# A gated cross-attention block with routed experts: the first batch's memsets, stack transfers and output bias are put elsewhere

## The chip, the cores and the metric
The kernel runs on one core of one Trainium2 chip. The metric is the device time of one execution in microseconds (us). Engines are named TensorE (PE in the profile; PEld is its weight load), VectorE (DVE), ScalarE (ACT), GpSimd (POOL) and SyncE (SP). SP, ACT and POOL can issue transfers (SPq, ACTq and POOLq in the rows, or a DMA row of POOL).

## The reference
32 batches of 112 query rows and 375 context rows, 256 wide, float32; 16 heads of 16.

```
x = x + tanh(g_xattn) * attention(layernorm(x), ctx, ctx)      # Wq, Wk, Wv, Wo with biases bq, bk, bv, bo
x = x + tanh(g_ffn) * experts(layernorm(x))                    # router: best 2 of 8, h = silu(x w1) * (x w3), y = h w2
```

## The kernel before
The program is written by hand: each engine has its own list of instructions, and semaphores order them across engines. There are two phases. In the first, the attention of 32 batches runs as a software pipeline of steps from i = -3 to 31. In the second, 63 tiles of 128 routed tokens go through the experts.

A step has 12 slots, k = 0 to 11. In step i the engines work on several batches: a = i + 3 is normed, turned and projected to queries and keys; s = i + 2 gets its values (L1168) and has its queries and keys stacked; c = i + 1 gets its score maxima (L1162 on TensorE, negated maxima by L869 on VectorE); b = i gets its exponents (L1130, L594); e = i - 1 gets its output. Batch 2 doesn't come in step -1 but between the steps -2 and -1 (third_batch). So batch 0 is projected in step -3, batch 1 in step -2, batch 2 behind it, and the maxima of batch 0 are taken in step -1.

Queries and keys are split in a high and a low part for exactness (the tile split, parts KHI, QHI, KLO, QLO). The parts of each head pair are then stacked under one another by transfers inside the SBUF: rows 0 to 31, 32 to 63 and 64 to 95 of the tile stack. Row 96 holds ones against the keys and the negated maxima against the queries. For each of four groups g of heads there are four transfers: from_high makes two (L280, L281), from_low two (L285, L286). For batches from 1 on SyncE issues all 16. For batch 0 SyncE issues 10 and GpSimd's stack_first 6 (L397 to L404). stacked(n) is the count that those who wait for a batch's stack compare with.

What stands around the change:
- GpSimd begins with constants, then the memsets of the ones rows, three of 1 x 3008 elements (L377), then a memset in v_sb (L379), then step -3 with queries(0) (L413 to L427), which masks and splits the queries, then stack_first. Its queue is in order.
- VectorE's first norm: statistics, half (L732), polish1 (L736 to L738) and the normed batch xn (L838). The roots between are on ScalarE (L544, L546).
- TensorE begins with 56 transposes of the identity as a warm-up (L1117), then turns the normed batch (L1247), which ScalarE copies (L610), and makes the queries (L1273) and keys (L1173).
- ScalarE issues the loads of Wo, bv, bo and the router weights, copies values (L567), turned batches (L610), queries (L621) and keys (L616). In third_batch its key copies (L660) wait for the stack of batch 0.
- The output bias: bo_gated = tanh(g) * (bo + bv Wo) is made once, in step -1: VectorE's L876 and L879, TensorE's L1304, VectorE's L883; at the same place the router weights are turned (L1297, L629). GpSimd adds bo_gated to a batch's rows of x one step ahead of their use; TensorE waits for it (s_bog) in step 0, before it writes the bank again.

## Time and profile before

| | us |
|---|---|
| median of 3 runs | 856.07 |
| lowest and highest | 853.0, 857.51 |
| the profiled execution's own time | 855.32 |
| its span in the profile | 853.6 |

| engine | busy us | share of the span |
|---|---|---|
| TensorE matmul | 825.3 | 97% |
| TensorE weight load | 673.7 | 79% |
| VectorE | 486.3 | 57% |
| ScalarE | 422.2 | 49% |
| GpSimd | 476.2 | 56% |

The profile is one execution with a time for each instruction. Matmuls overlap one another, so their row tells how long TensorE had work and not how well it was used. The mean granted clock of TensorE, in shares of 2.4 GHz, is 0.991 over the execution: it has two levels, 1.00 and 0.50 (1.2 GHz). A timeline row says when a group of instructions began, how long it lasted, on which engine and from which line of the kernel, and in square brackets how long the engine had stood idle before it and what ended that.

### The profile page before, as it was taken

How to read it: one execution, taken by the hardware profiler on the slowest of the kernel's cores; microseconds unless marked ns; L12 is line 12 of the kernel's file. 1: busy time of each engine (PE TensorE's matmuls, PEld its weight loads, DVE VectorE, ACT ScalarE, POOL GpSimd, SP SyncE). 2: the span in 40 equal slices, each digit the busy share in tenths (PEclk: the TensorE clock that was granted, in tenths of full speed). 3: DMA queues.
4: the chain of work that ended last, by engine and by line, in shares of the span. 5: the costliest groups of instructions: out<-in, count | busy, mean ns of one | idle time of the engine just before them, and what ended most of it. 6: DMA issues, size and time to landing. Idle time of an engine off the chain costs nothing.

```text
span 853.6 us, 21453 instructions
## 1 busy us (share of the span) xinstructions
PE 825.3 (97%) x7209; PEld 673.7 (79%) x7209; DVE 486.3 (57%) x1163; ACT 422.2 (49%) x1086; POOL 476.2 (56%) x570
## 2 busy tenths in 40 slices
PE   7899999999999999999999999899999999999995
PEld 6578888888888888888888888777777777777773
DVE  4566776777777776777787777655622222222221
ACT  2256665665666566656665666565222222222221
POOL 6454434454555555555655465455777766656652
PEclk8999999999999999999999999999999999999997
DMA  5876777776676677676656664574444443444432
GB/s 153 207 161 168 204 177 174 180 192 156 161 181 155 158 175 172 148 175 164 170 117 158 150 160 111 146 192 74 57 63 62 70 69 62 63 63 63 63 57 31
DMA packets 99842, 112.29 MB, mean 132 GB/s; under 512 B 29276, under 2 KB 81124, under 8 KB 99736
## 3 DMA queue, kind: packets, MB, share of 16 engines
q1 hardware_dynamic: 79720, 92.48, 45.1%
q0 software_dynamic: 18512, 17.60, 13.5%
q8 instruction: 61, 1.00, 0.6%
q10 hardware_dynamic: 1504, 0.85, 0.5%
q14 instruction: 45, 0.37, 0.2%
HBM read 35.48 MB, written 17.53 MB: 62 GB/s over the span
## 4 chain that ended last, share of the span: by engine, by line
PE 85%; DVE 11%; issue 2%; ACT 1%; DMA 1%; POOLq 0%; DVEq 0%; ACTq 0%
PE ps L1417 18%; PE ps L1173 10%; PE ps L1478 10%; PE ps L1162 9%; PE ps L1145 9%; PE ps L1130 8%; DVE negmax L869 6%; PE ps L1168 5%; PE ps L1273 3%; PE ps L1332 3%; PE ps L1436 2%; PE ps L1361 2%; PE ps L1265 2%; PE ps L1247 1%; DVE xa L854 1%
## 5 line engine op out<-in xcount | busy, mean ns | idle before, releaser
L869 DVE TENSOR_REDUCE negmax<-ps 112x2 f32<-112x750 f32 x256 | 240.1, 940 | 124.3 <-PE ps L1162 122.8
L594 ACT ACTIVATE probs<-ps 125x448 f32<-125x448 f32 x384 | 209.5, 547 | 101.8 <-PE ps L1130 95.6
L389 POOL DMA_DIRECT2D stack<-negmax_t x128 | 68.2, 536 | 228.5 <-ACT negmax_t L645 220.8
L1130 PE MATMUL ps<-stack 97*125 97x224 f32 x768 | 189.1, 328 | 0.9 <-ACT probs L594 0.4
L1130 PEld LDWEIGHTS ps<-stack 97*125 97x125 f32 x768 | 127.4, 188 | 28.1 <-ACT probs L594 1.5
L1162 PE MATMUL ps<-stack 96*112 96x376 f32 x512 | 136.7, 348 | 7.7 <-DVE negmax L869 5.4
L505 POOL DMA_INDIRECT out_dram<-y,idx x63 | 100.5, 1595 | 69.5 <-issue 34.4
L689 ACT ACTIVATE silu<-ps 128x352 f32<-128x352 f32 x63 | 29.3, 465 | 184.4 <-PE ps L1417 184.4
L1081 DVE TENSOR_TENSOR h<-silu,ps 128x352 f32<-128x352 f32 x63 | 32.8, 521 | 144.6 <-PE ps L1417 144.4
L1168 PE MATMUL ps<-wv_sb,ctx_t 128*125 128x256 f32 x384 | 100.0, 382 | 0.4 <-DVE split L859 0.4
L1173 PE MATMUL ps<-ctx_t,wk_sb 128*128 128x375 f32 x256 | 93.7, 489 | 0.7 <-ACT q_raw L654 0.7
L1478 PE MATMUL ps<-w_sb,h_t 128*128 x378 | 92.3, 380 | 0.7 <-ACT h_t L695 0.7
L1478 PEld LDWEIGHTS ps<-w_sb,h_t 128*128 128x128 f32 x378 | 71.7, 190 | 20.1 <-issue 0.9
L1417 PE MATMUL ps<-w_sb,xg_t 128*128 x252 | 84.9, 458 | 0.0
L1162 PEld LDWEIGHTS ps<-stack 96*112 96x112 f32 x512 | 72.0, 177 | 15.0 <-DVE negmax L869 13.9
L1145 PE MATMUL ps<-probs,v_sb 125*17 125x112 f32 x3072 | 79.8, 260 | 0.0
L1145 PEld LDWEIGHTS ps<-probs,v_sb 125*17 125x17 f32 x3072 | 71.7, 98 | 8.0 <-ACT probs L594 5.4
L496 POOL DMA_INDIRECT xg<-xn_scratch,idx x63 | 62.5, 992 | 25.4 <-issue 17.2
L567 ACT ACTIVATE v_sb<-ps 125x256 f32<-125x256 f32 x96 | 36.5, 381 | 78.8 <-PE ps L1145 76.6
L409 POOL DMA_INDIRECT slot_table<-pay,slots_i x64 | 64.2, 1003 | 15.3 <-issue 13.6
L1168 PEld LDWEIGHTS ps<-wv_sb,ctx_t 128*125 128x125 f32 x384 | 66.6, 187 | 6.8 <-DVE split L859 0.6
L1173 PEld LDWEIGHTS ps<-ctx_t,wk_sb 128*128 128x128 f32 x256 | 46.7, 195 | 18.3 <-issue 1.7
(221 smaller groups left out, 1216.9 us busy)
## 6 DMA issues: line engine op xcount, KB each, us to landing
stack<-split SPq DMA_DIRECT2D x252, 150.0 KB, 2.7
ctx_t<-in_ctx_dram SPq DMA_DIRECT2D x32, 375.0 KB, 3.9
stack<-split SPq DMA_DIRECT2D x127, 94.0 KB, 2.5
stack<-split SPq DMA_DIRECT2D x127, 56.0 KB, 2.1
out_dram<-xa SPq DMA_DIRECT2D x32, 112.0 KB, 3.5
xn_scratch<-xn SPq DMA_DIRECT2D x32, 112.0 KB, 3.3
xa<-in_x_dram SPq DMA_DIRECT2D x7, 448.0 KB, 5.6
w_sb<-in_L_ffn_w_dram SPq DMA_DIRECT2D x16, 176.0 KB, 3.1
```

The lines of the kernel that those rows point to most:

```text
L389: gp.dma_start(dst[:, :, SKP + SQ * h:SKP + SQ * h + SQ], negmax_t[4 * h:4 * h + 4, half, :].bitcast(f32)).then_inc(s_nmrow[half][c % NSLO ...
L409: gp.indirect_dma_start(table, bass.IndirectOffsetOnAxis(ap=slots_i[:, u % 2, GB * k + j:GB * k + j + 1], axis=0), pay[:, UNITS[u][j], k, ...
L505: gp.indirect_dma_start(out, bass.IndirectOffsetOnAxis(ap=idx[:, t % NI, 0:1], axis=0), y[:, t % NY, :], None, compute_op=ALU.add).then_in ...
L594: act.activation(probs[:, n % NP, :], ps[0:KW, EXPB + k % 2, 0:4 * SQ], ACT.Exp).then_inc(s_exp, 1)
L869: dve.tensor_reduce(negmax[:, half, :, p4], ps[0:SQ, m1:m2 + 1, 0:SK], axis=AX.X, op=ALU.max, negate=True).then_inc(s_max, 1)
L1130: last = pe.matmul(ps[0:KW, EXPB + k % 2, QW * m:QW * m + QW], stack[:, place_of(b), p, KW * ch:KW * ch + KW], stack[:, place_of(b), p, SK ...
L1145: last = pe.matmul(ps[32 * j:32 * j + HD + 1, PVB, SQ * g:SQ * g + SQ], v_sb[:, b % NSLOT, ch, head, :], probs[:, (12 * b + 3 * g + ch) % ...
L1162: last = pe.matmul(ps[0:SQ, max_banks(c, t)[h], 0:SKP], stack[0:ONE_ROW, place_of(c), t, SKP + SQ * h:SKP + SQ * h + SQ], stack[0:ONE_ROW, ...
L1168: last = pe.matmul(ps[0:KW, bank, 0:EMB], ctx_t[:, s % NSLOT, n, KW * ch:KW * ch + KW], wv_sb[:, n, :], start=(n == 0), stop=(n == DC - 1))
L1173: last = pe.matmul(ps[:, bank, 0:SK], wk_sb[:, n, P * m:P * m + P], ctx_t[:, a % NSLOT, n, :], start=(n == 0), stop=(n == DC - 1))
L1417: last = pe.matmul(ps[:, bank, 0:F], xg_t[:, t % NS, k, :], w[k][:, bass.ds(e, 1), :].rearrange("p e f -> p (e f)"), start=(k == 0), stop= ...
L1478: last = pe.matmul(ps[:, YB, 0:EMB], h_t[0:n, c, :], w2_sb[0:n, c, bass.ds(e_o, 1), :].rearrange("p e d -> p (e d)"), start=(c == 0), stop ...
```

## The change
- GpSimd waits for the first normed batch (s_xn at 1) before it writes the ones rows.
- The stack of batch 0 goes out on three queues: SyncE issues 8 transfers, GpSimd 5, and ScalarE 3 in a new stack_first of its own, right behind its step -3. It waits there for the low part of the queries of batch 0 (s_qlo) and its high keys (s_khi). The counts in stacked and in the waits for s_stack_gp follow.
- The output-bias chain and the turning of the router weights go from step -1 to step 0 on TensorE, VectorE and ScalarE; GpSimd's first three adds of bo_gated all come in step 1, and TensorE's wait for s_bog moves to step 1.
- TensorE makes four more identity transposes in step -3, between the turning of the first batch and its query matmuls.

```diff
         def stacked(n):
-            return 256 * (n // NSLOT + 1) - (96 if n % NSLOT == 0 else 0)
+            return 256 * (n // NSLOT + 1) - (80 if n % NSLOT == 0 else 0)
...
+                    def low_keys(g):
+                        rows, pr = slice(32 * g, 32 * g + 32), slice(DC * g, DC * g + DC)
+                        sp.dma_start(dst[32:64, pr, :], src[rows, :, KLO:KLO + KQ]).then_inc(s_stack[s % NSLOT], 16)
...
                         for g in range(2):
-                            from_low(g)
+                            low_keys(g)
...
             gp.wait_ge(s_split0, 1)
+            gp.wait_ge(s_xn, 1)
             for n in range(NSLOT):
                 gp.memset(stack[ONE_ROW:ONE_ROW + 1, n, :, 0:SKP].bitcast(f32), 1.0).then_inc(s_one, 1)
...
                 gp.dma_start(dst[32:64, pr, :], src[rows, :, KLO:KLO + KQ]).then_inc(s_stack_gp, 16)
-                gp.dma_start(dst[64:96, pr, :], src[rows, :, KHI:KHI + KQ]).then_inc(s_stack_gp, 16)
...
-                if c is not None and c > 0:
-                    if c == 1:
-                        gp.wait_ge(s_xn, 1)
+                if c is not None and c > 1:
+                    if c == 2:
                         gp.wait_ge(s_bog, 1)
-                        gp.tensor_tensor(xrow(0), xrow(0), bo_gated[:, :], ALU.add).then_inc(s_xb, 1)
+                        for n in range(2):
+                            gp.wait_ge(s_xn, n + 1)
+                            gp.tensor_tensor(xrow(n), xrow(n), bo_gated[:, :], ALU.add).then_inc(s_xb, 1)
...
-                    if k == 7 and i == -1:
+                    if k == 7 and i == 0:
                         act.wait_ge(s_wr_ps, 1)
...
+            def stack_first():
+                src, dst = split[:, 0, :, :].bitcast(f32), stack[:, place_of(0), :, :].bitcast(f32)
+                act.wait_ge(s_qlo, 1)
+                act.wait_ge(s_khi, DC)
+                for g in range(3):
+                    rows, pr = slice(32 * g, 32 * g + 32), slice(DC * g, DC * g + DC)
+                    act.dma_start(dst[64:96, pr, :], src[rows, :, KHI:KHI + KQ]).then_inc(s_stack[0], 16)
+
             for i in range(FIRST, LAST):
                 step(i)
+                if i == FIRST:
+                    stack_first()
...
-                    if k == 5 and i == -1:
+                    if k == 5 and i == 0:
                         dve.wait_ge(s_tanh, 1)
...
-                    if k == 9 and i == -1:
+                    if k == 9 and i == 0:
                         dve.wait_ge(s_bo_ps, 1)
...
-                            if i == 0:
+                            if i == 1:
                                 pe.wait_ge(s_bog, 1)
...
                         if a == 0:
+                            for n in range(4):
+                                pe.transpose(ps[:, 2, P * n:P * n + P], ident[:, :], ident[:, :])
                             pe.wait_ge(s_wq, 32)
...
-                    if k == 7 and i == -1:
+                    if k == 7 and i == 0:
                         pe.wait_ge(s_wr, 16)
-                        pe.wait_ge(s_nm_t, 1)
+                        pe.wait_ge(s_nm_t, 3)
...
-                    if k == 8 and i == -1:
+                    if k == 8 and i == 0:
                         pe.wait_ge(s_bvb, 1)
```

## Rows read from the trace of the kernel before

**Rows 1.** The page, part 1: busy us, share of the span, instructions.
```profile
PE 825.3 (97%) x7209; PEld 673.7 (79%) x7209; DVE 486.3 (57%) x1163; ACT 422.2 (49%) x1086; POOL 476.2 (56%) x570
```

**Rows 2.** Timeline, GpSimd, VectorE and ScalarE: start us, us, engine, line, operation, idle before.
```profile
2.10 7.72 POOL L377 MEMSET stack<- 1x3008 f32 x3
7.29 1.28 ACT L540 ACT_TABLE_LOAD   x1
8.33 1.52 DVE L732 TENSOR_SCALAR half<-mv 112x4 f32<-112x4 f32 x1
10.95 0.41 DVE L838 TENSOR_SCALAR xn<-xa,mv,rstd 112x256 f32<-112x256 f32 x1
...
43.00 0.17 DVE L732 TENSOR_SCALAR half<-mv 112x4 f32<-112x4 f32 x1
```

**Rows 3.** Timeline of TensorE from 1 to 26 us.
```profile
1.61 7.99 PE L1117 MATMUL ps<-ident 128*128 128x128 f32 x56 [1.61 <-POOL ident L364]
...
12.37 2.02 PE L1273 MATMUL ps<-xn_t,wq_sb 128*128 128x112 f32 x8 [0.54 <-ACT xn_t L610]
14.18 4.95 PE L1173 MATMUL ps<-ctx_t,wk_sb 128*128 128x375 f32 x8
...
21.96 1.04 PE L1273 MATMUL ps<-xn_t,wq_sb 128*128 128x112 f32 x8
...
24.40 1.43 PE L1173 MATMUL ps<-ctx_t,wk_sb 128*128 128x375 f32 x4
```

**Rows 4.** Windows: mean; busy (count) of PE, PEld, DVE, ACT, POOL; clock; DMA share, GB/s.
```profile
4.00:5.00 1.00, 1.00 (x7) 1.00 (x6) 0.73 (x1) 0.00 (x0) 1.00 (x2) 1.00 0.89 261
5.00:6.00 1.00, 1.00 (x11) 1.00 (x10) 0.00 (x0) 0.00 (x0) 1.00 (x1) 1.00 1.16 279
12.00:13.00 1.00, 0.64 (x3) 0.67 (x4) 0.28 (x1) 0.22 (x1) 0.00 (x0) 0.50 1.15 219
18.00:19.00 1.00, 1.00 (x4) 0.58 (x3) 0.53 (x1) 0.00 (x0) 0.52 (x1) 0.65 0.18 54
25.00:26.00 1.00, 1.00 (x5) 0.68 (x4) 0.00 (x0) 0.14 (x1) 1.00 (x3) 1.00 1.09 224
```

**Rows 5.** Timeline of GpSimd: the v_sb memset and the queries of batch 0.
```profile
9.88 0.36 POOL L379 MEMSET v_sb<- 125x144 f32 x1
15.20 0.56 POOL L422 TENSOR_TENSOR q_msk<-q_raw,q_mask 128x224 f32<-128x224 f32 x1 [4.97 <-ACT q_raw L621]
...
17.39 1.14 POOL L426 TENSOR_TENSOR split<-q_msk,split 128x448 fp32r<-128x448 f32 x1
```

**Rows 6.** Timeline: SyncE's first and last issue for batch 0, and who waited.
```profile
19.83 0.77 SPq L280 DMA_DIRECT2D stack<-split  x1
...
27.68 0.60 SPq L286 DMA_DIRECT2D stack<-split  x1
...
30.50 0.57 ACT L660 ACTIVATE split<-ps,bk_sb 128x375 fp32r<-128x375 f32 x1 [0.16 <-DMA stack<-split]
```

**Rows 7.** Timeline of ScalarE behind its step -3.
```profile
20.03 0.39 ACT L567 ACTIVATE v_sb<-ps 125x256 f32<-125x256 f32 x1 [0.29 <-PE ps L1168]
20.88 0.36 ACT L610 ACTIVATE xn_t<-ps 128x224 f32<-128x224 f32 x1 [0.47 <-PE ps L1247]
```

**Rows 8.** Step -1's end: timeline rows, and transfers of L389 to landing.
```profile
38.27 1.09 POOL L389 DMA_DIRECT2D stack<-negmax_t  x2 [4.39 <-ACT negmax_t L645]
38.38 1.09 PE L1304 MATMUL ps<-wo_sb,o_t 128*112 128x256 f32 x4 [0.36 <-ACT wr_t L629]
39.85 0.94 DVE L869 TENSOR_REDUCE negmax<-ps 112x2 f32<-112x750 f32 x1 [0.84 <-PE ps L1162]
40.71 0.48 DVE L883 SCALAR_TENSOR_TENSOR bo_gated<-ps,tanh_g,bo_gated 112x256 f32<-112x256 f32 x1
42.38 0.45 PE L1130 MATMUL ps<-stack 97*125 97x224 f32 x2
...
DMA to landing us min/median/max: 1.8/2.9/4.5
```

More of the change, by code:

```diff
@@ L415, in queries @@
                 if a == 2:
-                    gp.wait_ge(s_stack_gp, 96)
+                    gp.wait_ge(s_stack_gp, 80)
                 if a >= 2:
@@ L656, in third_batch @@
                 act.wait_ge(s_stack[0], stacked(0))
-                act.wait_ge(s_stack_gp, 96)
+                act.wait_ge(s_stack_gp, 80)
                 for m in range(DC):
@@ L1152, in maxes @@
                 if t == 0 and c == 0:
-                    pe.wait_ge(s_stack_gp, 96)
+                    pe.wait_ge(s_stack_gp, 80)
                 if c == B - 1 and t in (3, 4, 5, 6):
```

## The prediction
> **What bounds the kernel now.** I read the page first. TensorE's matmuls cover 97% of the span [rows 1]. So nearly every microsecond by which the first real step of TensorE moves is carried to the end, and the only open question is the start, where the change works. There I read the timelines engine by engine from 0 to 45 us, then the granted clock in 1 us windows, then the transfers.
>
> Three facts of the start matter. First, VectorE waits for GpSimd: the tiny half op of L732 takes 1.52 us while the third memset of the ones rows runs and ends just after it, and 0.17 us later in the kernel [rows 2]. The three memsets take 7.72 us together. Second, TensorE's warm-up ends at 1.61 + 7.99 = 9.60 us [rows 3], the first normed batch is ready only at 10.95 + 0.41 = 11.36 [rows 2], and after that pause the granted clock is 0.50, the 1.2 GHz level, from 12 to about 18.6 us [rows 4]. The first eight query matmuls cost 2.02 us instead of 1.04, the first eight key matmuls 4.95 [rows 3]. Third, GpSimd is free from 9.88 + 0.36 = 10.24 us on [rows 5], so that it takes the first queries at 15.20, as soon as they exist, and has both parts in split at 17.39 + 1.14 = 18.53 [rows 5].
>
> **The change part by part.**
>
> *Ones rows behind the normed batch.* On VectorE this gives back 1.52 - 0.17 = 1.35 us, of which ScalarE's table load, which ends at 7.29 + 1.28 = 8.57 [rows 2], leaves 1.3: the batch is normed at about 10.07 instead of 11.36. TensorE's pause shrinks from 1.8 to 0.5 us, so I expect the clock to stay at 2.4 GHz; that is worth (2.02 - 1.04) + (4.95 - 2 x 1.43) = 3.1 us [rows 3]. Together 4.4 us, early.
>
> But GpSimd's queue is strictly in order, and this is the step on which the forecast turns. The added wait on the normed batch holds back the three memsets, then the v_sb memset (0.36 us), then the queries of batch 0. Memsets: 10.1 to 17.8. v_sb: to 18.25. Queries: 3.33 us (15.20 to 18.53 [rows 5]), to 21.6. VectorE's second and third norming (0.41 us each [rows 2]) are of the kind that took turns with the memsets; each may add up to 0.4 to this row, so I take 22.0, with ends 21.6 and 22.4. The queries of batch 0 are therefore 3.5 us later than before.
>
> *Stack on three queues.* SP issues 8 transfers of batch 0 instead of 10, GpSimd 5 instead of 6, ScalarE 3 instead of none. The SP issues take 0.77 us at first and 0.60 and a gap later, from 19.83 to 28.28, and the last landed at about 30.5, when the copy of L660 went [rows 6]. All now starts when the queries are there, at 22.0. Lower bound for the landing: 8 issues of 0.65 and 2.7 to land, 8 us, so 30. Upper bound: as long as before, 10.7 us, so 32.7. The DMA engines were full already: share 1.09 at 224 GB/s [rows 4]. I take 9.5 us: 31.5, one later than before; it doesn't bound as long as the third batch is later too (below).
>
> The Trainium skill (Trainium Kernel Development and Optimization, Key Constraints) says that transfers issued from SP, ScalarE and GpSimd run on the same 16 DMA engines, and that issuing from several only saves issue time. The full share agrees; by the rule the three queues bring at most the two issues that SP is rid of, 1.3 us by the rows, and by itself it would change no sign.
>
> What the third queue costs is on ScalarE. Its stack_first stands between the first step and the second and waits for the queries. Queued behind it are the value copy of L567 and the copy of the turned second batch of L610, for which TensorE's queries of batch 1 wait. Before, they ran at 20.03 and 20.88 [rows 7]. Now: wait until 22.0, three issues of 0.8, 0.65 and 0.65, then 0.39 and 0.36 [rows 7] with small gaps: done at 25.05. The query matmuls of batch 1 start at 25.1 instead of 21.96: **3.1 us later**. All of the early 4.4 us lies in front of this wait and is lost in it: TensorE has the keys of batch 0, its first values and the first half of batch 1's keys done at about 19 and then stands for some 6 us.
>
> *The clock again.* Before, a pause of 1.8 us with little around it brought the 1.2 GHz level; one of 6 us will too. Work that began at 12.37 had the full clock at about 18.6; the warm-up, which began at 1.61, did 7 transposes in the microsecond from 4 and 11 in that from 5 [rows 3, 4]. By these two rises, 3.4 and 6.3 us after the first matmul, I take the clock back at 28.5 to 31.4. At half speed that costs 1.7 to 3.1 us, less what TensorE's short gaps up to 24.40 swallow (the eight queries end at 23.00 [rows 3], the values between take about 0.9 and leave 0.5), up to 1. I take 1.4, ends 0.7 and 3.1. The four identity transposes, 1/11 us each, lie in the 0.54 us in which TensorE waits for the turned batch [rows 3]: 0. If the clock were low there they would take 4/7 = 0.57, which is the gap as well; their help to the clock is in front of the same wait and lost with the rest.
>
> *Stack of batch 1.* It needs both keys of batch 1 low, at about 31, and SP free (28): 31 + 16 x 0.645 + 2.7 = 44; TensorE wants it (42.67 before) at 46 or later. Hidden by about 2 us.
>
> *Output-bias chain one step later.* Out of step -1 go two transposes, four matmuls (1.09 us and 0.36 of waiting for ScalarE [rows 8]), and VectorE's bo work, 0.48 us of it at the end. VectorE's idle 0.84 in front of the reduction at 39.85 goes. Upper bound of the gain: 0.84 + 0.48 + 0.36 = 1.7. But the next thing, the exponents of batch 0, needs the negated maxima in the stack: issued at 38.27 and done at 39.36, landing 1.8 to 4.5 us later; the exponents went at 42.35 [rows 8]. That landing was at 40.6 to 42.4 and doesn't move with this part. So the gain is 0 to 1.7; since the DMA engines are full here I take 0.5. Into step 0 goes the same work: TensorE there is nearly full, so 1.1 us, ends 0.8 and, with VectorE's last op of 0.48 on the way too, 1.6. GpSimd's adds go from two to three in the next step (0.75 us more), ahead of maxima that come 4 us later: 0. Net +0.6, ends -0.9 and +1.6.
>
> **Sum**, against the profiled execution (855.32 us, span 853.6, 1.7 outside): + 3.1 + 1.4 + 0.6 = + 5.1, so 860.4. That execution is 0.75 us below the median of the runs shown (856.07, runs from 853.0 to 857.51), so on the median it would be 861.2. I say 860.6.
>
> **Rivals.**
> - *The clock comes back at once or is never lost.* For: the old pause was followed by a nearly idle microsecond. Against: 6 us of nothing. + 3.1 + 0 to 0.6 - 0.9: 857.5 to 859.
> - *The clock stays low through the third batch.* The third batch has gaps of 0.4 to 0.9 us, and in the one recovery seen it took work without gaps. Another 8 query and 8 key matmuls at half speed, 3.5 us, and some of step -1: 863 to 866.
> - *The stack alone decides.* Before, the copy of L660 and the queries of batch 2 went just after the stack of batch 0 had landed (30.50 [rows 6]). If that landing was the true limit, only its own move counts: -0.4 to +2.2 us and the bias chain: 855 to 857.5. Against: the chain that ended last goes through keys and their copies there, and the keys were ready with it.
> - *Faster: GpSimd gets to the queries in time.* The place is GpSimd's queue. If the memsets behind the batch took at most 2 us instead of 7.72 (because their length before came from sharing with VectorE), queries and keys would meet at about 17, ScalarE would be rid of its issues at 19, and the queries of batch 1 would start at 19.7, 2.3 us earlier, at full clock: 852 to 854. It decides where GpSimd ends the ones rows before 13 us. Against: the memsets fill their 7.72 us evenly, also from 5 to 6 us, where VectorE ran nothing (VectorE 0.00, GpSimd 1.00 [rows 4]).
>
> **How the numbers follow.** Forecast 0.46 (858.8 to 862.5), clock kept 0.15, clock low long 0.18, stack alone 0.12, faster 0.09. The range leaves out the faster rival and the far end of the long one: 855.5 to 865.5. A measurement of this kernel can tell about 0.5%, 4.3 us, here up to 860.3: above it lie somewhat under two thirds of the forecast and all of the long rival, 0.48; below 851.8 lie the faster rival's far end and what I haven't seen, 0.07; within, 0.45.
>
> **What would show it.** In the changed kernel: the half op of L732 at about 0.17 us and the first normed batch at 10.1 (right: first part); the three memsets from 10.1 to 17.8 and the first queries of GpSimd at 18.3, not 15.2 (the step on which all turns); ScalarE's issues starting near 22 and L610's second copy near 24.7; TensorE idle from about 19 to 25; granted clock 0.50 somewhere from 20 to 30; the exponents of batch 0 at about 46.5. If GpSimd's queries come before 16 us, or ScalarE's copies before 21, the prediction is wrong on the side of faster.

## The result: slower, by more than predicted

| | us |
|---|---|
| changed kernel, median of 4 runs | 870.17 |
| lowest and highest | 868.57, 876.01 |
| kernel before, on the same chip | 856.79 |
| ratio, with its 95% interval | 1.0179 (1.013 to 1.0229) |
| the profiled execution's own time, its span | 876.01, 874.3 |

The change costs about 13 to 15 us. The prediction was 860.6 with a range of 855.5 to 865.5: the sign was right, the size was a third of the real one, and the time lies outside the range. Repeated with the experiments, the changed kernel gave 868.62 against 855.26, a ratio of 1.0152 (1.0122 to 1.0182), 13.0 us.

The page of the changed kernel, part 1 (busy us, share of the span, instructions), answers to [rows 1]:

```profile
PE 832.7 (95%) x7213; PEld 679.9 (78%) x7213; DVE 487.7 (56%) x1163; ACT 422.1 (48%) x1086; POOL 476.0 (54%) x569
```

TensorE is 7.4 us busier, though only four small instructions were added: the same work ran for longer at the low clock (mean granted clock 0.981 here, 0.991 before). The rest of the loss is waiting. Where both came in is seen by laying the marks of TensorE's timelines side by side. The turn of the maxima (L1178 before, L1193 in the changed kernel) comes once in every step:

| mark on TensorE | before | changed | later by |
|---|---|---|---|
| queries of batch 1 | 21.96 | 24.89 | 2.93 |
| maxima of batch 0 turned, step -1 | 37.06 | 41.37 | 4.31 |
| maxima of batch 1 turned, end of step -1 | 42.09 | 44.70 | 2.61 |
| first exponents (L1130, L1145) | 42.38 | 49.49 | 7.11 |
| next turn, end of that step's work | 50.32 | 58.63 | 8.31 |
| next turn, one step on | 58.31 | 72.41 | 14.10 |

To 540 us the difference stays at 14.4. It is 20.7 at the end of this execution (spans 874.3 and 853.6). The last 6.3 us belong to this execution, the longest of the four, more than to the change: the repeated kernel's profile has a span of 867.1, 13.5 above 853.6. So there are four pieces: +4.31, then -1.70, then +5.70, then +5.79, together 14.10.

**The first piece, +4.31.** Timeline of the changed kernel from 6 to 42 us, one engine after another (start us, us, engine, line, operation, count, idle before and what ended it), the part that answers to [rows 2], [rows 3], [rows 5] and [rows 7]:

```profile
8.39 0.17 DVE L747 TENSOR_SCALAR half<-mv 112x4 f32<-112x4 f32 x1
...
9.89 0.41 DVE L853 TENSOR_SCALAR xn<-xa,mv,rstd 112x256 f32<-112x256 f32 x1
10.81 2.37 DVE L853 TENSOR_SCALAR xn<-xa,mv,rstd 112x256 f32<-112x256 f32 x1 [0.51 <-PE ps L1262]
...
10.43 7.83 POOL L382 MEMSET stack<- 1x3008 f32 x3 [8.39 <-DVE xn L853]
18.79 0.56 POOL L426 TENSOR_TENSOR q_msk<-q_raw,q_mask 128x224 f32<-128x224 f32 x1
...
22.14 2.02 ACTq L673 DMA_DIRECT2D stack<-split  x3
24.20 0.38 ACT L572 ACTIVATE v_sb<-ps 125x256 f32<-125x256 f32 x1 [7.80 <-issue]
24.48 0.35 ACT L615 ACTIVATE xn_t<-ps 128x224 f32<-128x224 f32 x1
...
24.89 2.05 PE L1290 MATMUL ps<-xn_t,wq_sb 128*128 128x112 f32 x8 [6.05 <-ACT xn_t L615]
```

Read down, it is the chain of the prediction. The half op is fast and the first batch is normed at 10.30, but the memsets now follow it and push GpSimd's queries to 18.79 (15.20 before). They are done at 20.98 + 1.13 = 22.11. ScalarE's last copy ends at 16.40. It then waits 5.74 us, issues its three transfers from 22.14 on, and copies again at 24.20. The profile gives the 7.80 us between the two copies as idle and calls them "issue", since an issue isn't counted as work; the three issues lie within them. Then come the copy of the turned batch and, 0.06 us behind it, TensorE, after 6.05 us idle and at the low clock: eight queries take 2.05 us, not 1.04 [rows 3].

**The second and third piece, -1.70 and +5.70.** The same timeline around the end of step -1, GpSimd, SyncE and TensorE, and the transfers issued from 42.5 to 43.2 us (KB each, median us to landing), which answer to [rows 8]:

```profile
41.37 0.26 PE L1193 MATMUL ps<-ident,negmax 112*8 112x112 f32 x1
44.70 0.26 PE L1193 MATMUL ps<-ident,negmax 112*8 112x112 f32 x1 [0.23 <-DVE negmax L884]
49.49 0.73 PE L1145 MATMUL ps<-stack 97*125 97x224 f32 x2 [4.53 <-DMA stack<-negmax_t]
...
41.72 0.59 SPq L221 DMA_DIRECT2D ctx_t<-in_ctx_dram  x1
42.35 0.49 SPq L228 DMA_DIRECT2D xa<-in_x_dram  x1
...
42.58 1.08 POOL L394 DMA_DIRECT2D stack<-negmax_t  x2 [4.40 <-ACT negmax_t L650]
...
stack<-negmax_t POOLq DMA_DIRECT2D x2, 1.8 KB, 5.3
```

Between the two turns lie 3.33 us instead of 5.03: the bias chain is gone and has given back 1.70, all that the prediction had as its upper bound. But then TensorE waits 4.53 us for two transfers of 1.8 KB. SyncE has issued its next two loads, 375 and 448 KB, just ahead of them. In the kernel before GpSimd's pair was issued from 38.27 to 39.36 [rows 8], and the loads began 0.41 and 1.05 us behind its start:

```profile
38.68 0.59 SPq L221 DMA_DIRECT2D ctx_t<-in_ctx_dram  x1
39.32 0.50 SPq L228 DMA_DIRECT2D xa<-in_x_dram  x1
```

The order has turned round, because the maxima moved by 4.3 us and SyncE's loads by only 3.0. Of the 5.70 us, 4.50 have come in when the exponents start (7.11 - 2.61); the other 1.20 come in up to the next turn, where TensorE works at half speed at first (below).

**The fourth piece, +5.79.** Step 0 in the changed kernel, VectorE, GpSimd and TensorE from 58 to 73 us:

```profile
59.69 0.35 DVE L891 TENSOR_SCALAR bo_gated<-bo_sb,tanh_g 112x256 f32<-112x256 f32 x1
60.07 0.47 DVE L894 TENSOR_SCALAR o_t<-head_rows,bv_col 128x112 f32<-128x112 f32 x2
60.45 2.48 DVE L751 TENSOR_TENSOR lnt<-lnr 112x4 f32<-112x4 f32 x1
62.96 0.16 DVE L752 TENSOR_TENSOR lnt<-lnt,half 112x4 f32<-112x4 f32 x1
63.15 0.99 DVE L753 SCALAR_TENSOR_TENSOR rstd<-lnt,lnr 112x4 f32<-112x4 f32 x1
64.17 0.94 DVE L884 TENSOR_REDUCE negmax<-ps 112x2 f32<-112x750 f32 x1
...
60.78 0.57 POOL L426 TENSOR_TENSOR q_msk<-q_raw,q_mask 128x224 f32<-128x224 f32 x1
61.31 0.56 POOL L427 TENSOR_TENSOR split<-q_raw,q_mask 128x224 fp32r<-128x224 f32 x1
61.83 0.56 POOL L426 TENSOR_TENSOR q_msk<-q_raw,q_mask 128x224 f32<-128x224 f32 x1
62.34 0.55 POOL L427 TENSOR_TENSOR split<-q_raw,q_mask 128x224 fp32r<-128x224 f32 x1
62.97 1.15 POOL L430 TENSOR_TENSOR split<-q_msk,split 128x448 fp32r<-128x448 f32 x1
...
65.17 0.59 PE L1177 MATMUL ps<-stack 96*112 96x376 f32 x2 [1.48 <-DVE negmax L884]
66.80 0.97 PE L1177 MATMUL ps<-stack 96*112 96x376 f32 x2 [0.82 <-DVE negmax L884]
```

In the kernel before, the polish and the first masking op stood so:

```profile
51.38 0.15 DVE L736 TENSOR_TENSOR lnt<-lnr 112x4 f32<-112x4 f32 x1
52.49 0.57 POOL L422 TENSOR_TENSOR q_msk<-q_raw,q_mask 128x224 f32<-128x224 f32 x1
```

The polish of L751 handles 4 numbers in each of 112 rows. It takes 0.15 us in the kernel before and 2.48 us here. It ends at 62.93, when GpSimd's fourth masking op ends (62.34 + 0.55 = 62.89). L753 takes 0.99 and ends at 64.14, with GpSimd's next op (64.12). In the kernel before the polish had just passed in front of the masking. The bias ops, 0.35 + 0.47 us ahead of it, push it against the masking, the next reduction comes only at 64.17, and TensorE stands for it. That is 5.54 us behind the turn at 58.63; in the kernel before the same reduction starts at 52.34, 2.02 us behind its turn. So 3.52 of the 5.79 us have come in there. The other 2.27 come in behind it, most of that time at the low clock.

**The clock.** Windows of the changed kernel (mean; busy and count of PE, PEld, DVE, ACT, POOL; granted clock; DMA share, GB/s), answering to [rows 4]:

```profile
22.00:30.00 8.00, 5.12 (x17) 4.12 (x18) 1.51 (x5) 2.08 (x6) 5.34 (x11) 0.57 0.79 196
46.00:54.00 8.00, 4.24 (x16) 3.67 (x16) 1.71 (x3) 1.83 (x5) 0.85 (x2) 0.57 0.92 211
66.00:74.00 8.00, 7.20 (x38) 5.97 (x42) 4.14 (x7) 2.71 (x6) 0.54 (x1) 0.57 0.42 93
584.00:600.00 16.00, 12.67 (x148) 10.14 (x147) 4.47 (x20) 6.35 (x18) 6.47 (x7) 0.89 0.64 156
```

A mean of 0.57 over 8 us is 0.50, the 1.2 GHz level, for most of it. In windows of 1 us the clock is at 0.50 from about 22.4 to 29.0, from 46.0 to 52.9 and from 66.5 to 73.2 us, some 7 us each time. The first two stretches begin within the long waits (6.05 and 4.53 us), so TensorE works at half speed for only 4.1 and 3.4 us of them; the third begins behind the two shorter waits (1.48 and 0.82), and in it TensorE works almost all the time. The last row lies where attention hands over to the experts, and belongs to the late 6.3 us. The kernel before had one such stretch at its start [rows 4] and none from 20 to 76 us.

### The profile page after: what moved, and what is told of

Same layout as the page of the kernel before. It is cut to its first block, busy times and chain, and to the rows that moved or that the text cites. A ratio compares the mean times of both kernels' runs of the same rounds, so it can differ in the third digit from the quotient of the medians.

```text
span 874.3 us, 21463 instructions
## 1 busy us (share of the span) xinstructions
PE 832.7 (95%) x7213; PEld 679.9 (78%) x7213; DVE 487.7 (56%) x1163; ACT 422.1 (48%) x1086; POOL 476.0 (54%) x569
## 4 chain that ended last, share of the span: by engine, by line
PE 82%; DVE 10%; DMA 2%; issue 2%; POOL 2%; ACT 1%; ACTq 0%; POOLq 0%; DVEq 0%
PE ps L1434 17%; PE ps L1495 9%; PE ps L1177 9%; PE ps L1160 9%; PE ps L1188 9%; PE ps L1145 7%; PE ps L1183 6%; DVE negmax L884 5%; PE ps L1290 3%; PE ps L1349 3%; PE ps L1453 2%; PE ps L1378 2%; PE ps L1280 1%; DVE xa L869 1%; PE ps L1262 1%
## 5 line engine op out<-in xcount | busy, mean ns | idle before, releaser
L1145 PE MATMUL ps<-stack 97*125 97x224 f32 x768 | 191.2, 332 | 5.3 <-DMA stack<-negmax_t 4.5
L1145 PEld LDWEIGHTS ps<-stack 97*125 97x125 f32 x768 | 129.1, 190 | 32.9 <-issue 5.7
L1183 PE MATMUL ps<-wv_sb,ctx_t 128*125 128x256 f32 x384 | 104.3, 395 | 0.0
L1188 PE MATMUL ps<-ctx_t,wk_sb 128*128 128x375 f32 x256 | 91.7, 480 | 0.7 <-ACT q_raw L659 0.7
L1183 PEld LDWEIGHTS ps<-wv_sb,ctx_t 128*125 128x125 f32 x384 | 69.3, 194 | 6.8
L1434 PEld LDWEIGHTS ps<-w_sb,xg_t 128*128 128x128 f32 x252 | 47.3, 188 | 16.9
```

The lines of the kernel that those rows point to most:

```text
L1145: last = pe.matmul(ps[0:KW, EXPB + k % 2, QW * m:QW * m + QW], stack[:, place_of(b), p, KW * ch:KW * ch + KW], stack[:, place_of(b), p, SK ...
L1183: last = pe.matmul(ps[0:KW, bank, 0:EMB], ctx_t[:, s % NSLOT, n, KW * ch:KW * ch + KW], wv_sb[:, n, :], start=(n == 0), stop=(n == DC - 1))
L1188: last = pe.matmul(ps[:, bank, 0:SK], wk_sb[:, n, P * m:P * m + P], ctx_t[:, a % NSLOT, n, :], start=(n == 0), stop=(n == DC - 1))
L1434: last = pe.matmul(ps[:, bank, 0:F], xg_t[:, t % NS, k, :], w[k][:, bass.ds(e, 1), :].rearrange("p e f -> p (e f)"), start=(k == 0), stop= ...
```

## The experiments

Three causes were on trial, called A, B and C. **A:** the wait in front of the memsets delays GpSimd's queries and, through ScalarE's new wait, the second batch. **B:** the loads of SyncE, issued ahead of GpSimd's pair of maxima, delay the landing. **C:** the bias chain in step 0 meets GpSimd's masking. Every kernel below computes all that the reference asks for; only places and orders differ. Ratios are to the kernel before, measured on the same chip in the same rounds, with their 95% interval. I turn a ratio into us with the median of the kernel before beside it, some 855 to 861.

**The ones rows alone** (kernel before, one line added).

```diff
             gp.wait_ge(s_split0, 1)
+            gp.wait_ge(s_xn, 1)
             for n in range(NSLOT):
```

> The kernel before with one edit: GpSimd waits for the first normed batch before it writes the ones rows. Theory A (GpSimd's queue order): the memsets run from 10.4 to 18.3 us and the low part of the queries of batch 0 is ready at 22.1 instead of 18.53. ScalarE isn't held here, so TensorE's queries of batch 1 start early, near 18.6 instead of 21.96; but the stack of batch 0 starts 2.3 us later (22.2) and lands near 32.8, the key copies of the third batch wait for it, TensorE stands some 4 us, and the first reduction of step -1 starts at 34.7 to 36.5 instead of 33.09. Total +2 to +5 us, and up to +9 if the loads that SyncE issues behind the stack of batch 1 get ahead of the negated maxima. Rival (the memset costs only together with ScalarE's new transfers): the early gain of 3 us stays, total -3 to 0 us.

Measured: 861.09 us, ratio 1.0043 (1.002 to 1.0067), 3.7 us slower. Timeline, GpSimd, ScalarE and TensorE:

```profile
18.66 0.56 POOL L423 TENSOR_TENSOR q_msk<-q_raw,q_mask 128x224 f32<-128x224 f32 x1
...
32.11 1.04 ACT L661 ACTIVATE split<-ps,bk_sb 128x375 fp32r<-128x375 f32 x2 [3.49 <-DMA stack<-split]
...
47.44 0.45 PE L1131 MATMUL ps<-stack 97*125 97x224 f32 x2 [0.80 <-DMA stack<-negmax_t]
```

GpSimd's queries come as late as in the whole change. Without ScalarE's new wait the second batch goes early (its queries at 18.80), but the key copies of the third then wait 3.49 us for the late stack, so the delay comes out a little further on. There the granted clock falls too: it is at 0.50 from about 31 to 45 us. The first reduction, at 33.75, is only 0.7 us later than before, but the first exponents are 5.1 us later. The wait in front of the memsets is a cost by itself, whichever queue carries the stack.

**The three queues alone** (kernel before with stack_first on ScalarE, SyncE 8, GpSimd 5).

```diff
+            def stack_first():
+                src, dst = split[:, 0, :, :].bitcast(f32), stack[:, place_of(0), :, :].bitcast(f32)
+                act.wait_ge(s_qlo, 1)
+                act.wait_ge(s_khi, DC)
...
+                if i == FIRST:
+                    stack_first()
```

> The kernel before with one part of the change: stack of batch 0 on three queues (SyncE 8, GpSimd 5, ScalarE 3). Theory B (order of issues): ScalarE waits only until 19.7 for its own key copies and issues for 2 us, so that the first reduction of step -1 starts 0.6 to 1 us later. SyncE is free 1.3 us earlier, so its loads of context 3 and of x are issued near 38.1 to 38.8, in front of GpSimd's transfers of the negated maxima (38.9 instead of 38.27), and these land 5 to 6 us after issue instead of within 3: the first exponents 3 to 5 us later, with low clock behind it. Total +3 to +7 us. Rival (landing time doesn't depend on that order): total +0.5 to +1 us.

Measured: 859.72 us, ratio 1.0035 (1.0016 to 1.0053), 3.0 us slower. Timeline around 36 us, all engines:

```profile
36.24 0.59 SPq L221 DMA_DIRECT2D ctx_t<-in_ctx_dram  x1
...
36.45 1.09 POOL L393 DMA_DIRECT2D stack<-negmax_t  x2 [4.27 <-ACT negmax_t L648]
...
36.87 0.50 SPq L228 DMA_DIRECT2D xa<-in_x_dram  x1
...
43.96 0.52 PE L1143 MATMUL ps<-stack 97*125 97x224 f32 x1 [3.44 <-DMA stack<-negmax_t]
```

This is B with neither of the others. SyncE, rid of two issues, is at its loads 0.2 us ahead of GpSimd's pair, and the first exponents wait 3.44 us. Step 0 is untouched (53.37 to 61.37, 8.0 us). The edit that was meant to shorten the stack costs through what SyncE does next. The clock is at 0.50 from about 42 to 49 us, within and behind this wait.

**The bias chain alone** (kernel before, the conditions `i == -1` of the bias and the router turned to `i == 0`, GpSimd's adds as in the change).

```diff
-                    if k == 5 and i == -1:
+                    if k == 5 and i == 0:
                         dve.wait_ge(s_tanh, 1)
```

> The kernel before with one part of the change: the output-bias chain and the turning of the router weights in step 0 instead of -1. Theory C (VectorE and GpSimd get in each other's way in step 0): the last reduction of step -1 ends 1.7 us earlier, the first exponents come 0 to 1.7 us earlier; in step 0 the polish of the norm (two operands in SBUF), pushed back by 0.8 us of bias work, meets GpSimd's masking of the queries and lasts 2 to 3.5 us instead of 0.5; step 0 becomes 3 to 5 us longer. Total +2 to +5 us. Rival (only its own work moves): step 0 +1.1 to +1.6 us, total -0.6 to +1.6 us.

Measured: 863.65 us, ratio 1.0073 (1.0047 to 1.0099), 6.2 us slower, the dearest part. Timeline, VectorE and TensorE:

```profile
52.00 2.38 DVE L737 TENSOR_TENSOR lnt<-lnr 112x4 f32<-112x4 f32 x1
...
40.19 0.45 PE L1131 MATMUL ps<-stack 97*125 97x224 f32 x2 [1.76 <-DMA stack<-negmax_t]
```

The 1.70 us gained in step -1 (turns at 34.84 and 38.17) turn into 1.76 us of waiting for the maxima, as the prediction had feared. The prediction didn't reckon with what follows: behind this wait the clock is at 0.50 from about 42 to 48 us, and from the exponents to the next turn it takes 9.90 us (40.19 to 50.09), not 7.94. Step 0 takes 50.09 to 62.85, 12.76 us instead of 7.99, and the polish takes 2.38. So two thirds of this part's loss are step 0, and the rest is the low clock behind the wait. The three parts alone cost 3.7 + 3.0 + 6.2 = 12.9 us, the whole 13.0; each of the three carries some 2 us of uncertainty, so the close agreement is chance in part.

**The loads behind the maxima** (changed kernel, SyncE's loop in step -1).

```diff
+                if i == -1:
+                    sp.wait_ge(s_nmrow[0][0], 32)
                 if a is not None and NSLOT - 1 <= a < B - 1:
```

> The changed kernel, and SyncE waits in step -1 for the landing of batch 0's first negated maxima before it issues the loads of context 3 and of x. Theory B (the 1.8 KB transfers landed 6.2 us after issue because 823 KB of loads were issued just ahead of them): they land within 3.5 us, TensorE's stall of 4.5 us before the first exponents shrinks to at most 1.5, the granted clock stays at 1.00 there; 4 to 6 us faster than the changed kernel in the same runs. Rival (GpSimd's transfers land late by themselves, or because of the stack transfers of batch 1): stall of 3.5 us or more as before, no gain.

Measured: 862.86 us, ratio 1.005 (1.0031 to 1.0068). Timeline, GpSimd and SyncE, and the transfers issued from 43.5 to 44.8 us:

```profile
43.62 1.09 POOL L396 DMA_DIRECT2D stack<-negmax_t  x2 [4.40 <-ACT negmax_t L652]
...
45.81 0.37 SPq L221 DMA_DIRECT2D ctx_t<-in_ctx_dram  x1
...
stack<-negmax_t POOLq DMA_DIRECT2D x2, 1.8 KB, 1.6
```

The pair lands in 1.6 us instead of 5.3, the exponents go at 45.92 with no wait, and the clock is kept there. From turn to turn it is 45.74 to 53.97, 8.23 us, exactly as in the kernel before (42.09 to 50.32). So the third piece is B's. Step 0 stays bad (13.78 us), as it should. Against 1.0152 this is 1.0%, 8.7 us, of which the timeline shows 5.7; I expected 4 to 6. The two ratios are from different chips and their intervals allow for it.

The edit holds back SyncE's whole queue, the next stack transfers included (46.80 instead of 42.96), so this run alone doesn't tell the loads from those. The two kernels before it do: in both the next stack transfer is issued more than 1 us behind the pair's start (37.49 against 36.45, and 37.59 against 36.05). Only the loads stand otherwise: the first 0.21 us ahead of the pair with the three queues, 0.29 us behind it with the bias chain moved. From the pair's issue to the exponents it is 7.51 us in the one and 4.14 in the other.

**The changed kernel again, and the polish ahead of the bias ops.** The first is the reference point for the polish and for the copy of the ones rows, on one chip.

> The changed kernel itself, for a ratio beside the others on the same chip. All theories: 8 to 15 us slower than before; the stall of 4 to 5 us before the first exponents and the polish of 2.5 and 1 us in step 0 are there again. The extra 5 us between the attention and the experts, seen once, is expected in few executions.

Measured: 868.62 us, ratio 1.0152, with a wait of 3.72 us in front of the first exponents and a step 0 of 12.75 us (58.72 to 71.47). In the second, polish1 was put in front of the bias block of VectorE's slot k = 5.

```diff
+                    if k == 5 and i % GB == 0 and 1 <= i // GB + 1 < NG:
+                        polish1(i // GB + 1)
                     if k == 5 and i == 0:
```

> The changed kernel with VectorE's polish of the norm put in front of the bias work in step 0. Theory C (the polish, with two operands in SBUF, was pushed by 0.8 us of bias work into GpSimd's masking of the queries and waited for it): the polish takes 0.16 us an operation, step 0 is 3 to 4 us shorter, and the clock doesn't fall around 66 us; 4 to 6 us faster than the changed kernel. Rival (the bias work itself, 1.2 us on VectorE and 1.1 on TensorE, makes step 0 long): at most 1 us faster.

Measured: 869.96 us, ratio 1.0167 (1.0137 to 1.0196): no gain at all. Timeline, VectorE and TensorE:

```profile
59.19 0.15 DVE L751 TENSOR_TENSOR lnt<-lnr 112x4 f32<-112x4 f32 x1
...
60.16 2.51 DVE L896 TENSOR_SCALAR o_t<-head_rows,bv_col 128x112 f32<-128x112 f32 x2
...
62.73 2.00 PE L1321 MATMUL ps<-wo_sb,o_t 128*112 128x256 f32 x4 [2.04 <-DVE o_t L896]
```

The polish is back at 0.15 us and my expectation fell: now the bias op stands beside GpSimd's masking (60.30 to 62.40) and takes 2.51. TensorE waits 2.04 us for it, its next scores are late, and with them VectorE's next reduction, at 67.39 after 3.87 us of waiting. Step 0 takes 58.14 to 71.51, 13.4 us. What is in conflict is then not one op but the place: 0.82 us more of VectorE's work has to fit in front of GpSimd's masking of batch 3. Step -1 had no such masking. The run was meant to part the conflict from the work itself (the rival) and doesn't, since the conflict only went over to another op.

**The ones rows by a copy** (changed kernel, no wait on the first batch, no long memset: GpSimd sets 8 x 376 elements, and SyncE copies them three times).

```diff
-            gp.wait_ge(s_xn, 1)
-            for n in range(NSLOT):
-                gp.memset(stack[ONE_ROW:ONE_ROW + 1, n, :, 0:SKP].bitcast(f32), 1.0).then_inc(s_one, 1)
+            gp.memset(one_src[:, :], 1.0).then_inc(s_one_src, 1)
...
+            for n in range(NSLOT):
+                sp.dma_start(stack[ONE_ROW:ONE_ROW + 1, n, :, 0:SKP].bitcast(f32), one_src[:, :]).then_inc(s_one, 16)
```

> The changed kernel with the ones rows made in another way: GpSimd writes a small source of 8 x 376 ones (about 0.35 us instead of 7.8) and SyncE copies it into row 96 three times. Theory A (GpSimd's memsets in front of the queries hold ScalarE): GpSimd takes the queries at 12.8, SyncE and ScalarE start the stack at 16.5, TensorE's queries of batch 1 start at 19 to 20 instead of 24.9 and with full clock; the first reduction of step -1 starts 6 to 8 us earlier, at 29.5 to 31. What is left of the loss is B and C. 6 to 8 us faster than the changed kernel. Rival (the stack's transfers on a full DMA bound the third batch): first reduction at 34 or later.

Measured: 863.15 us, ratio 1.0098 (1.0069 to 1.0127), 4.6 us better than the changed kernel on the same chip. Timeline, ScalarE and TensorE:

```profile
16.74 2.09 ACTq L676 DMA_DIRECT2D stack<-split  x3
...
19.56 1.15 PE L1293 MATMUL ps<-xn_t,wq_sb 128*128 128x112 f32 x8 [0.59 <-ACT xn_t L618]
```

With GpSimd free, its queries come at 13.37, ScalarE issues from 16.74, and the queries of batch 1 go at 19.56 instead of 24.89, with the clock at 1.00. The first reduction comes at 30.50 instead of 38.01. A is confirmed: ScalarE's wait was dear only because what it waits for was late. I expected 6 to 8 us. The timeline has 6.3 of them at the end of step 0 (65.13 against 71.47), the ratios 4.6, with some 3.6 us of uncertainty. The clock is at 0.50 here from 33 to 37 us, where the changed kernel kept it. B (3.68 us) and C (step 0 from 52.39 to 65.13) are still there.

**The bias chain back in step -1** (changed kernel, the reverse of the bias edit above).

> The changed kernel with the output-bias chain and the router turning back in step -1. Theory C as it stands after the run with the polish in front (whatever of VectorE's two-port work stands in step 0 behind 59 us meets GpSimd's masking of the queries, and the bias chain puts TensorE behind it): step 0 lasts 8 to 8.5 us between its two turnings of the maxima, not 13; the polish 0.16 us an operation; 3.5 to 6 us faster than the changed kernel of the run before (ratio 1.015 to the kernel before), so 1.008 to 1.011. The stall before the first exponents (B) is there, of 2 to 3.5 us, since the last reduction is 1.7 us later. Rival (step 0 was long through the low clock and the late landing in front of it): step 0 stays over 11 us.

Measured: 868.27 us against 861.25 on this chip, ratio 1.0074 (1.005 to 1.0098). Timeline of TensorE:

```profile
58.89 0.26 PE L1192 MATMUL ps<-ident,negmax 112*8 112x112 f32 x1
...
66.88 0.26 PE L1192 MATMUL ps<-ident,negmax 112*8 112x112 f32 x1
```

Step 0 is 7.99 us again and the polish 0.15, although the wait before the exponents (2.66 us) and the low clock behind it are still there: the rival is out. By the ratios the chain's move costs 0.8%, 6.7 us, within the whole change, and 6.2 alone. That its place in step 0 costs this is shown both ways. That it costs through the meeting with GpSimd's masking is read from the rows (2.38 to 2.51 us where 0.15 and 0.47 stood); no run keeps the chain in step 0 and takes the masking away, so the share of the chain's own work isn't measured.

**All three undone** (changed kernel with the ones rows by a copy, the loads behind the maxima and the bias chain back; the three queues and the four transposes stay).

> The changed kernel with all three named causes taken away: ones rows by a copy (A), SyncE's loads behind the landing of the negated maxima (B), bias chain back in step -1 (C). The stack on three queues and the four transposes stay. If A, B and C are the whole account: first reduction at 30 to 31, no wait of TensorE on a transfer before the first exponents, step 0 of 8 to 8.5 us, ratio to the kernel before 0.995 to 1.001. If something else in the change costs: ratio above 1.003.

Measured: 858.97 us against 861.25, ratio 0.9974 (0.9951 to 0.9996). Timeline of TensorE at the end of step -1:

```profile
39.60 0.26 PE L1197 MATMUL ps<-ident,negmax 112*8 112x112 f32 x1 [1.06 <-DVE negmax L888]
```

The exponents follow at 39.70 with no wait, the next turns are at 47.83 and 55.83, and the granted clock is 1.00 in every window from 4 to 76 us. So nothing of the 13 us is left that A, B and C don't cover. What is left of the change gains about 2 us together with the copy and the later loads. The copy takes more away than the wait in front of the memsets, since the memsets go as well. So the fair measure for the three queues and the four transposes is the kernel before with the same copy and later loads (next, 0.9987): against it they gain 1.1 us, which the intervals don't tell from nothing. Undone one at a time the three give 4.6, 8.7 and 6.7 us, 20 in all, against 15.3 for all at once; those differences each carry some 3 us of uncertainty, and I don't claim how they overlap.

**Attempts at a better kernel.** The kernel before with the ones rows by a copy and the loads behind the maxima:

> The kernel before with two edits: ones rows by SyncE's copy as above (GpSimd is free from 2.3 us on and never stands in VectorE's way in the first norm), and SyncE's loads of step -1 behind the landing of batch 0's first negated maxima. All theories agree that the first norm is 1.3 us earlier and the clock isn't lost at 12 us; the early gain of 3 us should carry to the end, since nothing stands in its way: first reduction at 29.5 to 30.5, first exponents at 39, 2 to 3.5 us faster than before, less in executions in which the kernel before keeps its clock at the start. If it isn't faster, something behind the start is fixed in time and the account of the loss misses it.

Measured: 854.84 us against 855.26, ratio 0.9987 (0.9975 to 0.9999). The first reduction comes at 30.39 (33.09 before), but the turn at 49.65 is only 0.7 us early (50.32): the clock was at 0.50 from about 33 to 41 us and took the gain back. I expected 2 to 3.5 us and got 1.1 (0.1 to 2.1). Next, ScalarE's six issues of loads were also moved behind its two key copies:

> The kernel before with ones rows by a copy, SyncE's loads behind the landing, and ScalarE's six load issues of step -3 put behind its two key copies. The keys of batch 0 are copied at 14 instead of 15.4, as soon as they are made, so the first reduction starts at 28.8 to 29.3, 1.2 us earlier than without the last edit. Total 1 to 2 us better than that kernel (ratio 0.9987): 0.996 to 0.998, if the clock isn't lost more often.

Measured: 861.48 us, ratio 0.9994 (0.9981 to 1.0006), no gain, again an expectation missed. The key copies are earlier, but the issues (15.45 to 18.33) then stand in front of the copy of the turned batch at 18.66, and TensorE's queries of batch 1 go at 19.07 where they went at 19.26. Last, three identity transposes, which change no result, were put in front of each score group of batch 0 but the first:

> The kernel of the third run of this call, and TensorE makes three identity transposes into a bank that is free there in front of each of its waits for a reduction in step -1 (21 transposes, 0.09 us each at full clock). If the low clock from 33 to 41 us in the run with ones rows by copy came from TensorE's waits in this step, the clock stays at 1.00 there: 0.5 to 2 us better than without, ratio 0.994 to 0.997. Rival (the work of the transposes lies in TensorE's way and the clock falls in other places anyway): no better, up to 1 us worse.

Measured: 861.11 us, ratio 0.9984 (0.9966 to 1.0002). Window from 33 to 41 us, without the transposes:

```profile
33.00:41.00 8.00, 7.41 (x23) 5.34 (x21) 4.77 (x9) 0.71 (x3) 1.09 (x2) 0.57 0.64 149
```

With them:

```profile
33.00:41.00 8.00, 6.91 (x42) 5.59 (x40) 6.52 (x16) 1.78 (x6) 1.43 (x3) 1.00 0.68 167
```

They kept the clock at 1.00 where it was 0.57, and the first exponents went at 39.62 instead of 41.53. The whole execution gained less than can be told apart from nothing: between 564 and 580 us, where attention hands over to the experts, the clock dipped again in both (mean 0.89 with the transposes, 0.79 without). Of all these kernels the one with the three parts undone has the lowest ratio, 0.9974; its interval overlaps with those of the last three.

## Why the prediction was wrong, point by point

- *Ones rows on VectorE:* right. The half op took 0.17 us, the first batch was normed at 10.30 (predicted 10.07), the clock stayed at 1.00 at first.
- *Memsets in GpSimd's queue:* right. They ran 10.43 to 18.26 (predicted 10.1 to 17.8), and the queries were done at 22.11 (predicted 22.0). One term in it was right by luck: the 0.4 us for VectorE's two normings didn't come in, since the memsets took 7.83 us instead of 7.72. It was VectorE that paid, with 2.37 and 0.82 us for ops of 0.41. The memsets' start, 0.33 us later than predicted, made up for it.
- *ScalarE's wait:* right. Issues at 22.14, the copy at 24.48, TensorE's queries at 24.89 (predicted 22.0, near 24.7, 25.1), 2.93 us late against 3.1 predicted. With the clock term, 3.1 + 1.4 = 4.5, this is the piece measured as 4.31. This clock term was right too: the granted clock was low behind this wait and back at 29.0 us (predicted 28.5 to 31.4), before the third batch (queries in 1.04 us). Its working was weaker than its outcome: the rise that it read from 7 and 11 transposes is none of the granted clock, which is 1.00 in both rows [rows 4]. And the 4.31 holds against this one execution of the kernel before, which had lost its clock at the start; see the last section.
- *The stack of batch 0 on three queues:* right that it doesn't bound. The key copies of batch 2 don't wait for it, while they do wait 3.49 us in the kernel with the ones rows moved and the old queues. *Four transposes:* right, 0.60 us inside a gap. *Stack of batch 1:* hidden, as said.
- *The output-bias chain:* here the prediction failed. Its term was "Net +0.6, ends -0.9 and +1.6". What it was to cover, from the turn at 41.37 to that at 72.41, measured -1.70 + 5.70 + 5.79 = +9.8 us. The chain by itself cost 6.7 us within the whole change and 6.2 alone; most of the 5.70 belongs to the order of issues, for which no term stood. Two statements in it were wrong.
  - "That landing was at 40.6 to 42.4 and doesn't move with this part". I took the landing's bounds from the rows of the kernel before [rows 8] and didn't look at what was issued beside it. GpSimd's pair went 0.4 us ahead of the first of two loads of 823 KB together. After my own forecast the maxima move by 4.5 us; how far SyncE's loads move I never worked out. They move by 3.0, and the order is reversed. Strictly, this failure is of the sum of all parts, since the three queues alone do it: 3.44 us of waiting. (The exponents went at 42.38 and not at 42.35, as the prediction reads [rows 8]; that changes nothing.)
  - "TensorE there is nearly full, so 1.1 us". I priced the work moved by its duration and asked only whether TensorE had room. The question to ask was who runs beside VectorE at that moment. The row of L426 in [rows 5] shows the kind of op, and the rows of L732 in [rows 2] had already shown what a small VectorE op costs beside GpSimd. I used that for the start and not for step 0: the 1.1 us put down for it measured 5.79.
- *The rival of a clock low for long* came nearest (863 to 866, still below the 870), and for a wrong reason: the clock did come back for the third batch, and then fell twice more, at two waits that I hadn't foreseen. The rivals "clock kept", "stack alone" and "faster" did not happen; the last fell at its own point, since the memsets took 7.83 us wherever they stood.
- *The range* left out 866 and more because every term was bounded within one mechanism. No term stood for a new wait in the step after the edits. The 860.6 itself lies between the two sums, 860.4 and 861.2, and no reason is given for it; at this distance from 870 it doesn't matter.

The Trainium skill (SBUF — State Buffer, section "SBUF: two separate sides") says that a pair of ports shared by VectorE and GpSimd is an exclusive lock: for the kinds of op that it names, whichever starts first has it for the whole instruction, and the other is blocked. The three rows of 2.38, 2.48 and 2.51 us agree as to the blocking. They differ from it or go beyond it in two things. VectorE's op stayed blocked over four GpSimd instructions of 0.55 us each, and was let in at none of the three boundaries, where GpSimd's rows overlap by some 0.04 us. And by the rows VectorE's op had begun 0.14 to 0.33 us ahead of the first of them and still was the one that waited (60.45 against 60.78 in the changed kernel); the runs don't show what held it in that time.

## What to carry to other kernels

A wait in front of work in an in-order queue is paid by everything behind it, so follow that queue until it is level with the old one, also into the queue that the next edit lets wait on it. Before an edit that shifts steps by a few microseconds, list the transfers issued within one or two microseconds of every small transfer that somebody waits for, and work out for both sides how far they move: the order of issue is part of the schedule. When VectorE's work is moved, look at GpSimd's row at the new moment and not only at TensorE's room, and put a price of its own on the low clock behind each new wait.

## What the runs showed of the hardware

- A pair of GpSimd transfers of 1.8 KB landed in 1.6 us when nothing large was issued ahead of it, and in 5.3 us with 375 and 448 KB issued within 0.9 us ahead. Counted from the pair's issue to the exponents that waited for it: 4.14 us with the bias chain alone moved, where the pair was issued 0.3 us ahead of the loads, and 6.1 to 7.5 us in the seven kernels where it came behind the first load or both. That the order sets this time is shown; how the transfers share the engines isn't.
- A VectorE op on 112 x 4 elements took 2.38 and 2.48 us over four back-to-back GpSimd ops with two operands, and 0.15 alone; VectorE's reductions, which read PSUM, took 0.94 us beside the same GpSimd ops and alone. Beside the memsets, the second norming took 2.37 us and ended after the first of three (10.43 + 7.83 / 3 = 13.04, against 13.18).
- The stretch of low clock at the very start of the kernel before is not in each execution: the kernels with only the three queues and only the bias chain moved have the same start, kept 1.00 in the windows from 4 to 36 us and had their first reduction at 31.25 and 30.86 instead of 33.09. So the first piece would be about 2 us larger against an execution that kept its clock.
